# New step tables for the last two iterations, a tile table built by GpSimd, plain padding writes and two early row loads

## What is computed

```python
def _L0_xattn_ref(q, k, v, Wq, bq, Wk, bk, Wv, bv, Wo, bo):     # 16 heads of 32
    ...
    scores = jnp.einsum('bhqd,bhkd->bhqk', qh, kh) * scale
    attn = jax.nn.softmax(scores, axis=-1)
    out = jnp.einsum('bhqk,bhkd->bhqd', attn, vh)
    concat = out.transpose(0, 2, 1, 3).reshape(B, LQ, D_MODEL)
    return concat @ Wo + bo

def _L0_ffn_ref(x, gate_w, expert_w):                           # 8 experts
    scores = jnp.einsum('bsh,eh->bse', x, gate_w)
    chosen = jnp.argmax(scores, axis=-1)
    onehot = jax.nn.one_hot(chosen, gate_w.shape[0], dtype=x.dtype)
    expert_out = jnp.einsum('bsh,efh->bsef', x, expert_w)
    return x + jnp.einsum('bsef,bse->bsf', expert_out, onehot)

x = x + _L0_xattn_ref(_layernorm(x, axis=-1), ctx_512, ctx_512, ...)
x = x + _L0_ffn_ref(_layernorm(x, axis=-1), gate_w, expert_w)
```

## Time and profile before

| | us |
|---|---|
| median of 3 runs | 975.7 |
| lowest and highest | 975.64, 977.84 |
| the profiled execution's own time | 974.32 |
| its span (first to last instruction) | 972.2 |

### The profile page before, as it was taken

One profiled execution on the slowest core, in us unless ns is written; L12 is line 12 of the kernel. 1 busy time (PEld: TensorE's weight loads), 2 busy tenths in 40 slices (PEclk: granted clock), 3 DMA queues, 4 the chain that ended last, 5 costly groups with the idle time before them and its releaser, 6 DMA issues. The chain is left out here.

```text
span 972.2 us, 27544 instructions
## 1 busy us (share of the span) xinstructions
PE 905.9 (93%) x8838; PEld 546.2 (56%) x8839; DVE 779.4 (80%) x1812; ACT 556.4 (57%) x928; POOL 530.6 (55%) x565
## 2 busy tenths in 40 slices
PE   5999999999899999899999999999775999999995
PEld 3446666556565665566556566566643555555552
DVE  8997999989699998879999889887793555555553
ACT  4686867768578686676867768657631111111110
POOL 2425454654546546455564554635552777777774
PEclk9998999999999999999999999998887999999998
DMA  9323142443424425233342542229233555555550
GB/s 316 98 69 108 39 138 75 135 124 75 134 62 138 120 72 150 68 122 102 97 143 59 146 106 65 78 67 327 77 131 98 169 170 172 163 167 167 174 174 21
DMA packets 81447, 119.51 MB, mean 123 GB/s; under 512 B 20465, under 2 KB 45797, under 8 KB 81327
## 3 DMA queue, kind: packets, MB, share of 16 engines
q1 hardware_dynamic: 68207, 81.63, 31.1%
q0 software_dynamic: 12048, 36.28, 9.9%
q10 hardware_dynamic: 1072, 0.02, 0.1%
HBM read 55.24 MB, written 38.13 MB: 96 GB/s over the span
## 5 line engine op out<-in xcount | busy, mean ns | idle before, releaser
L535 POOL TENSOR_TENSOR p_lo<-pf,p_hi 77x512 f16<-77x512 f32 x128 | 148.1, 1162 | 210.5 <-ACT p_hi L1128 210.2
L1127 ACT ACTIVATE pf<-scoresT,exp_scale 77x512 f32<-77x512 f32 x256 | 174.4, 681 | 73.2 <-PE scoresT L860 60.7
L1630 PE MATMUL mo<-e_w,x2T_hi 128*128 x576 | 184.5, 382 | 0.7 <-DVE x2T_lo L1667 0.7
L1128 ACT ACTIVATE p_hi<-scoresT,exp_scale 77x512 f16<-77x512 f32 x256 | 174.8, 683 | 0.0
L1650 ACT ACTIVATE x2T_hi<-mt 128x512 f16<-128x512 f32 x72 | 43.0, 597 | 183.4 <-PE mt L1619 183.4
L1677 DVE SCALAR_TENSOR_TENSOR res<-mo,inv,row 128x512 f32<-128x512 f32 x72 | 54.1, 751 | 91.6 <-PE mo L1630 91.6
L535 DVE TENSOR_TENSOR p_lo<-pf,p_hi 77x512 f16<-77x512 f32 x128 | 103.2, 822 | 14.8 <-ACT p_hi L1128 13.4
L1215 DVE TENSOR_REDUCE negmax<-work 128x4 f32<-128x308 f32 x256 | 112.6, 468 | 0.3 <-PE work L912 0.3
L1630 PE MATMUL mo<-e_w,x2T_lo 128*128 x288 | 110.1, 382 | 0.0
L1601 POOL DMA_INDIRECT out<-res,row x72 | 71.5, 993 | 65.4 <-DVE xn L1662 57.1
L832 PE MATMUL work<-wo_hi,cT_hi 128*128 128x512 f16 x256 | 97.3, 380 | 0.7 <-DVE cT_lo L1193 0.6
(11 more groups left out here) (257 smaller groups left out, 2179.5 us busy)
## 6 DMA issues: line engine op xcount, KB each, us to landing
row<-rows_by_expert SPq DMA_DIRECT2D x72, 257.5 KB, 3.0
q_st<-q_hi SPq DMA_DIRECT2D x256, 64.0 KB, 2.0
xt<-in_x SPq DMA_DIRECT2D x15, 1024.0 KB, 7.4
q_st<-q_lo SPq DMA_DIRECT2D x128, 64.0 KB, 2.0
ebuf<-in_L_ffn_expert_w SPq DMA_DIRECT2D x14, 512.0 KB, 8.3
er<-in_L_ffn_expert_w SPq DMA_DIRECT2D x7, 1024.0 KB, 14.9
out<-res,row POOLq DMA_INDIRECT x72, 2.8
xt<-in_x SPq DMA_DIRECT2D x4, 256.0 KB, 6.2
```

What stands on the lines that cost most here:

```text
L535: return tt.tensor_tensor(pp[1][0:LK, g % 2, j, :], pf[:, j, :], pp[0][0:LK, g % 2, j, :], ALU.subtract)
L1127: nc.scalar.activation(pf[:, j, :], sbank[n % SB][0:LK, :], ACT.Exp, scale=exp_scale[0:LK, :])
L1128: nc.scalar.activation(pp[0][0:LK, g % 2, j, :], sbank[n % SB][0:LK, :], ACT.Exp, scale=exp_scale[0:LK, :]).then_inc(sem("exp_done"), 1)
L1630: ins = nc.tensor.matmul(obank2[u % 2][:, :], x2T[ia][:, u % 2, k, :], w, start=k == 0 and n == 0, stop=k == KT - 1 and n == 2)
```

## The change

1. **New last tables.** Six of the twelve E steps of the last core iteration go to the closing iteration. PV0 to PV3, R and GC stand earlier or in other places between the scores. The closing iteration begins with one E step ahead of C0.
2. **Padding by plain transfers.** POOL's eight indirect transfers are gone. SP reads the eight ends from `pads` into a register, one after the other, and writes 128 rows from `zrow` at each. `pads` is now a cast of `base`, without the addition of the row number.
3. **Tile table on POOL.** TA on DVE ends after four instructions. POOL makes the sums over experts in three steps, with one tile per partition (`pair`, `cols`), 14 small instructions in all. PE then transposes the two columns (step TT) and DVE copies them to `tab` with one instruction. TB is gone.
4. **Last rows in halves.** VE of the last chunk is split into VF0 and VF1; POOL makes the row factors and the scatters of two tiles at a time.
5. **Two early row loads.** SP reads two table entries before it waits for the scatters, and loads two tiles ahead of the barrier. The other six first loads stand behind the barrier, at the start of SP's part of the expert loop.

The core of the diff (not shown: buffer names, the split of `scatter` and `load_rows` into helpers, and the new `VECTOR_LAST` and `SCALAR_LAST` tables, which follow `STEPS_LAST`):

```diff
 STEPS_LAST = order("""
-    NM C0 C1 C2 C3 O0 S00 S01 O1 S02 S03 O2 S10 S11 GC O3 S12 S13 E00 E01 S20 S21 R PV0 E02 E03 S22 S23 E10 E11
-    PV1 S30 S31 E12 E13 S32 S33 E20 E21 PV2 E22 E23 PV3
+    NM C0 C1 C2 C3 O0 S00 S01 O1 S02 GC S03 S10 O2 R S11 S12 O3 S13 E00 E01 PV0 S20 S21 S22 E02 S23 PV1 E03 S30 E10
+    E11 S31 S32 S33 PV2 PV3
 """)
 VECTOR_END = order("""
-    C0 C1 C2 C3 E30 O0 B0 E31 GC H E32 O1 B1 R PD SL E33 TA O2 B2 E40 E41 O3 B3 VE TB E42 E43 E50 E51 E52 E53
-    E60 E61 E62 E63 E70 E71 E72 E73
+    E12 C0 C1 C2 C3 E13 E20 E21 GC H O0 R PD TA E22 E23 B0 O1 E30 B1 VF0 E31 SL O2 E32 O3 B2 B3 E33 VF1 E40 E41 E42
+    E43 E50 TT E51 E52 E53 E60 E61 E62 E63 E70 E71 E72 E73
 """)
...
-            sp.wait_ge(sem("table_ready"), 1)
-            sp.wait_ge(sem("padded"), 16 * (E + 1))
+            sp.wait_ge(sem("pads_ready"), 1)
+            sp.wait_ge(sem("pool_experts"), ZEROS_MADE)
+            for e in range(E):
+                end = sp.value_load(pads[0:1, e:e + 1], min_val=0, max_val=E * REGION)
+                sp.dma_start(rows[bass.ds(end, P), :], zrow[:]).then_inc(sem("region_ended"), 16)
+            sp.wait_ge(sem("work_used"), use(Chunk(B - 1, CPB), "TT") + 1)
+            firsts = [first_row(sp, u) for u in range(NAHEAD)]
+            sp.wait_ge(sem("padded"), 16)
+            sp.wait_ge(sem("region_ended"), 16 * E)
             for par in range(2):
                 sp.wait_ge(sem(f"scattered{par}"), 16 * TPC * (NCHUNK // 2) + 16)
-            for u in range(UNROLL):
-                load_rows(sp, u, u)
+            for u in range(NAHEAD):
+                load_rows(sp, firsts[u], u)
...
-            pool.wait_ge(sem("pads_ready"), 1)
-            for e in range(E):
-                nc.gpsimd.indirect_dma_start(
-                    out=rows, out_offset=bass.IndirectOffsetOnAxis(ap=pads[:, e:e + 1], axis=0),
-                    in_=zrow[:], in_offset=None).then_inc(sem("padded"), 16)
+            pool.wait_ge(sem("tiles_counted"), 1)
+            do(nc.gpsimd.tensor_copy(sums[0][:, 4:], nti[:]))
+            nc.gpsimd.tensor_scalar(jump[:], sums[0][:, 4:], -float(P), float(REGION), ALU.mult, ALU.add)
+            for n in range(3):
+                do(nc.gpsimd.tensor_tensor(sums[n + 1][:, 4:], sums[n][:, 4:], sums[n][:, 4 - 2 ** n:4 + E - 2 ** n],
+                                           ALU.add))
+            do(nc.gpsimd.tensor_scalar(pair[:, 1, :], sums[3][:, 4:], row_p[:], None, ALU.is_le))
+            do(nc.gpsimd.tensor_tensor(pair[:, 0, :], pair[:, 1, :], jump[:], ALU.mult))
+            do(nc.gpsimd.tensor_tensor(pair[:, :, 0:4], pair[:, :, 0:4], pair[:, :, 4:8], ALU.add))
+            do(nc.gpsimd.tensor_tensor(pair[:, :, 0:2], pair[:, :, 0:2], pair[:, :, 2:4], ALU.add))
+            do(nc.gpsimd.tensor_tensor(cols[:], pair[:, :, 0], pair[:, :, 1], ALU.add))
+            do(nc.gpsimd.tensor_scalar(start[:], row_p[:], float(P), None, ALU.mult))
+            do(nc.gpsimd.tensor_tensor(cols[:, 0:1], cols[:, 0:1], start[:], ALU.add))
+            do(nc.gpsimd.tensor_scalar(cols[:, 0:1], cols[:, 0:1], float(E * REGION), None, ALU.min))
+            nc.gpsimd.tensor_scalar(cols[:, 1:2], cols[:, 1:2], float(E - 1), None, ALU.min)\
+                .then_inc(sem("columns_ready"), 1)
             last = Chunk(B - 1, CPB - 1)
-            row_factors(last, pool, do)
-            scatter(last, pool)
+            par = last.slot % 2
+            for half in range(2):
+                two = slice(2 * half, 2 * half + 2)
+                wait_alone(pool, "ln2_half", half + 1)
+                do(nc.gpsimd.tensor_tensor(pay[:, par, two, C_RSTD], ve2[:, two], pows[:, 0, two], ALU.pow))
...
+                wait_alone(pool, "slot_ready", last.n + 1)
+                for t in (2 * half, 2 * half + 1):
+                    scatter_tile(par, t)
...
+                if kind == "TT":
+
+                    pe.wait_ge(sem("columns_ready"), 1)
+                    for n in range(2):
+                        ins = nc.tensor.transpose(ps[0:1, n * P:(n + 1) * P], cols[:, n:n + 1], ident[:])
+                    return ins
...
+                if kind == "TT":
+                    return nc.vector.tensor_copy(
+                        tab[0:1, :, :], ps[0:1, 0:2 * P].rearrange("p (a t) -> p a t", a=2)[:, :, 0:NTILE])
...
         @blk.sync
         def _(sp):
+            for u in range(NAHEAD, U):
+                load_rows(sp, first_row(sp, u), u)
```

93 lines of the change are left out of this document (45 added, 48 removed).

## The result

| | before | after |
|---|---|---|
| median, us (first comparison, 4 runs each) | 976.33 | 965.73 (963.88 to 966.26) |
| ratio, 95% interval | 1 | 0.9889 (0.9872 to 0.9906) |
| median, us (second comparison, 7 and 4 runs) | 976.76 | 965.21 (963.44 to 966.23) |
| ratio, 95% interval | 1 | 0.9877 (0.9861 to 0.9894) |
| the profiled execution's own time and span, first comparison | 974.32, 972.2 | 966.26, 964.4 |

A forecast was written before the change was run, and what follows sets the result against it. It took the idle hand-over before PE's expert loop, DVE's closing work and the last core iteration's chain as what the change could shorten: -5.5 - 1.9 - 6.2 = -13.6 us, giving 962.1 us from the median, range 958.0 to 966.5.

The forecast's parts named there:

- (a) The hand-over: Between DVE's last E step and the first `xn`: the gap falls from 6.95 to 0.75 us, -6.2.
- The other path: Last rows, from POOL's scatters through SP's loads to the first `xn`: ready at 724.2, 1.7 us ahead of the barrier.
- (b) The closing iteration: Last `cT_lo` to DVE's last E step: less DVE work, -1.9 us, bounds -2.5 and -0.5.
- (c) The last core iteration: Chain over ACT, POOL, PE and DVE to C0: three pieces get shorter, -5.5 us, C0 at 689.3.
- S20's exponential: Last core iteration: PE's new order starts it near 675.3 instead of 676.29, -1.0 us, bounds 0 and -1.5.
- From there to the end of S33: ACT's gapless stretch in the last core iteration: four of six E steps go at 0.6 us, -2.4 us.
- From there to C0: End of S33 to C0: no E steps ahead of V20 and V21, 5.77 to 3.7 us, -2.1, bounds -1 and -2.5.
- POOL's table and TT: Closing iteration: 14 instructions at 0.3 us, 4.2 us, columns at 705, no cost if there before about 716.5.
- The clock: PE's first expert tile runs at the lower clock, 3.1 us left in; rival that it stays up: 959.0, chance 0.10.
- The code fetch: Rival at the barrier between the programs: DVE's branch must fetch code, 3.3 us lost, 965.4; chance 0.07.
- The last rows bound: Rival at the hand-over: POOL's second half starts or lands too late, 1 to 3 us lost, 963 to 965; chance 0.10.
- The idle before `xn`: Sign at the hand-over: DVE's idle time before its first `xn` under 1.5 us in the profile after.

The follow-up runs named there:

- r2: Changed kernel with POOL's drain left out at the barrier between the two programs: 962.16 us, ratio 0.9844.
- r4: Changed kernel without POOL's waits for the landing of scattered and padding rows at the first program's end, drain kept: 962.14 us.
- r8: Changed kernel with the tile table made by DVE again, without POOL's fourteen instructions and step TT: 969.40 us.
- r1: The changed kernel run again without any edit, as measure for the others: 965.21 us.
- r7: Changed kernel with the padding written by eight indirect transfers of POOL again, ahead of its table: 971.90 us.
- r9: Changed kernel with the last four tiles' rows in one piece again, VE instead of VF0 and VF1: 968.36 us, ratio 0.9904.
- r6: Changed kernel with the old tables of the last core iteration and six E steps less in the closing iteration: 968.33 us.
- r12: r11 with POOL's x+bo of the fourth tile moved ahead of P02 in the last core iteration: 953.65 us, ratio 0.9752.
- r10: Changed kernel without POOL's middle drain and with eight instead of two row loads ahead of the barrier: 965.70 us, ratio 0.9873.
- r5: The kernel before with POOL's drain left out at the barrier between the programs: 977.42 us against 976.51, ratio 1.0002.
- r3: Changed kernel with POOL's drain left out at both barriers, middle and end: 955.32 us, ratio 0.9781.
- r11: r3 plus ten matmuls on PE around the middle barrier whose results nobody reads: 953.83 us, ratio 0.9762.

## Why the prediction was right and where it was wrong

**(a) The hand-over: -6.2 forecast, -3.06 and -3.46 measured** (6.95 and 7.35 against 3.89 twice). This is the step that failed. It said "The first is the barrier: DVE's end at 725.1 plus 0.65 us, as after SP now, plus 0.1 for DVE to drain". Two paths were named, and a third one was there: POOL's last issue, 2.8 us for its landing, 6.5 us of drain. Nothing in the timelines of the five engines shows it, but the line of the block does, in the profile of before too. The whole remaining difference (3.89 to 0.58) goes when the drain goes (r2), or when POOL comes to it earlier (r4). The 0.65 us after SP was right as a price, once DVE really is last (0.58 in r2, 0.53 in r8).

**The other path.** The last row loads were 1.7 us ahead of the barrier in the forecast. In r1 SP issues them from 723.52, 3.2 us before DVE's last E step ends (726.68). So the path of the rows was right as to SP, and wrong as to what else hangs on POOL: what POOL's last scatter is late by comes out at the first `xn` with no air (7.3 us late, 7.3 us lost in r7; 4.3 and 3.8 in r9). This is why r7 and r9 cost 7.3 and 3.8 us from A to D and not "under a microsecond" and what exceeds 1.7. The sum of this path has a slip too: 720.9 + 2.9 is 723.8 and not 724.2, so the air that it gave was 2.1 us and not 1.7.

**(b) The closing iteration: -1.9 forecast, -4.0 measured** (32.5 to 28.5 from B to C). The direction was right and two terms were mis-sized. First, the price of an E step. I took 9.89 / 14 = 0.706 from the earlier trace rows for five more steps, 3.5 us; in the profile after they go at 7.33 / 11 = 0.667. In the kernel before, DVE did TB from 718.46 on and gave back none of PE's four buffers, so PE stood for 5.73 us, its clock fell, and some of the 14 steps had to wait for a PE at 1.2 GHz (in the stretch shown DVE is busy 0.80 us of one, PE all of it, at a mean clock of 0.56):

```profile
723.40 4.51 PE L919 MATMUL work<-ident,er 128*128 128x128 f32 x24 [5.73 <-DVE e_w L1183]
```

```profile
726.00:727.00 1.00, 1.00 (x8) 1.00 (x7) 0.80 (x3) 0.78 (x2) 0.72 (x1) 0.56 0.47 181
```

With 25 steps at 0.667 instead of 20 at about 0.70 it is +2.7 us. Second, I added 0.5 us for waits on PE "that the table work used to cover". They did not come: DVE stood 1.7 us for PE's output products in r1, and 1.9 before. r6 shows the other side of it: the E steps cover part of those waits. These two make 1.3 us of the 2.1 missing; the rest I can't assign.

**(c) The last core iteration: -5.5 forecast, -3.8 measured** in the first pair of profiles: from A to C0 on PE, 694.80 - 655.04 = 39.76 before, 695.47 - 659.49 = 35.98 after. By its three pieces:
- S20's exponential, forecast -1.0: it starts at 676.29 - 655.04 = 21.25 from A before and at 680.61 - 659.49 = 21.12 after, -0.1. The walk gave DVE's `oh` its 0.19 us of before; it took 2.17, since GC and H now meet POOL's `p_lo` and x+bo. r12 got back part of ACT's wait behind it (1.22 us instead of 2.43).
- From there to the end of S33, forecast -2.4: 12.74 before, 691.66 - 680.61 = 11.05 after, -1.7. ACT is no longer gapless: it stands 0.49 us until 688.10 for a score of PE, whose granted clock is 0.50 from 685 to 687.
- From there to C0, forecast "3.7 us: -2.1": 695.47 - 691.66 = 3.81, -2.0. Right.

C0 to the last `cT_lo`, taken as unchanged, got 0.4 us shorter (5.00 to 4.63).

**Costed at nothing, rightly.** POOL's table and TT: PE was not held at TT (columns at 710.33, TT at 718.97), and the price of 0.3 us an instruction held (3.9 us for fourteen). SP's padding was off the path as said (8.05 us from 706.71, nobody asked before 725). The third `xn` waited 0.20 us for its row and PE for nothing.

**The clock.** Left in with 3.1 us, and it stayed in: PE stood 6.41 us and not 3.2, the clock fell within the us from 728, and the first tile began at 1.2 GHz in both profiles of after (`mt` 1.97 us for two tiles' transposes, as before). How long it stayed low differs: from the first `xn` to the second tile's `mt` it is 8.32 us before, 7.67 after and 8.61 in r1.

**The rivals.** The code fetch, with 965.4, named nearly the measured time and is wrong (r2). That its 3.3 us are near the drain's 3.31 (3.89 less 0.58) is an accident. "The last rows bound" came nearest in kind, since it is POOL's last scatters that count, but by the drain and not by the rows. The sum -5.5 - 1.9 - 6.2 = -13.6 came out as -3.8, -4.8 and -3.1, together -11.6 before rounding, in the first pair (the 0.4 us behind C0 counted with the closing iteration), and as -10.6 and -11.6 in the two comparisons of the time. The gain was forecast 3.1 us too large at the hand-over, 1.7 too large in the core iteration and 2.9 too small in the closing one. That the time came within 3.6 us of the point, and inside the range, is partly luck: two errors of 4.9 us in sum met one of 2.9 the other way.

**The signs it named.** The idle before `xn` was to be under 1.5 us and was 3.89: that sign failed, and it is the one on the step that was wrong. The last scatter was not to be issued after 721; its issue begins at 721.35 in the first profile of after, but that profile's A is 4.45 us later than before, and in r1 it begins at 719.66. With the same 4.45 taken off, C0 comes at 691.0 instead of 689, POOL's columns at 705.9 (706 to 708 was said), and the first `xn` at 727.8 instead of at most 727. PV3 starts 0.1 us behind POOL's last `p_lo`, and SP's two loads go out before DVE's last E step ends, as said.

**Undoing the parts one by one** gives +3.0 (tables), +7.3 (padding), +3.1 (table), +3.8 (halves) from A to D against the mean of the two profiles of after, 17 us, and the whole change is worth 11.8. They don't add up, and the last scatter shows it already: undone one by one they move it by 2.9, 7.3, 1.8 and 4.3 us from A, 16 together, while in the kernel before it is 9.4 us later. Undone at once, POOL's longer work and DVE's later results would run beside each other; that is argued, since no run undoes two parts.

## What to carry to other kernels

Before counting an engine's end as the end of a barrier, read the sequencers' records of the block's own line: each engine's drain and the semaphore behind it. In these kernels POOL's drain took 5.9 to 7.3 us at both barriers, it started only when POOL came to it, and the loads on SP hid it completely until they were moved. Let POOL reach its drain early (let another engine wait for the landing), or leave the drain out where all its transfers are waited for; both gave 3.1 us here. And a price taken from a row holds only for that row's conditions: the 0.706 us of an E step contained a PE that the removed work itself had held up and slowed.

## What the runs showed of the hardware that I had not expected

- **POOL's drain:** 6.52 us in the middle where SP writes the padding (after, r1, r6, r8, r9), 7.27 and 7.17 where POOL sends it by eight indirect transfers (before, r7). DVE's record of 1.20 us in the same barrier ends with DVE's last work, and SP's is 0.13. Begun before the landing, POOL's ends 6.6 us after the last issue (r4), so it does not start over at the landing.
- **Its length remembers what POOL sent long before.** At the kernel's end it is 5.93 us wherever the middle drain stands. Without that one it is 6.36 (r2, r10), and 7.01 in r5, whose POOL also sent the eight padding transfers some 250 us earlier: the eight add 0.65 us there, as they add 0.65 to 0.75 in the middle. So the length follows what was sent since the last drain, at least in part; what it does in that time is open.
- **Left out at the kernel's end,** the drain gives back its whole length (6.36 us in r2) in the time too: 6.8 us (r3 against r2).
- **A DVE step of 0.19 us took 2.17** while POOL read two inputs from SBUF, and ended within 0.05 us of the end of POOL's second instruction (r11): it was held over two of POOL's instructions in a row. With the second of them moved away, it took 0.96 (r12).
- **Row loads with register values read early** go out every 0.51 us (r10), against 1.0 us with the read in between the earlier trace rows.
